# All four feature strips in one matrix call over four PSUM banks, with new orders on every engine

## What is computed

```python
x = x + tanh(g_xattn[0]) * performer(layernorm(x), ctx, ctx, random_features)   # causal, 16 heads of 8, 32 features
x = x + tanh(g_ffn[0])   * channel_mix(layernorm(x), W_r, W_k, W_v, mu_r, mu_k)   # sigmoid gate, squared relu
x = x + tanh(g_xattn[1]) * gated_cross_attention(ctx, layernorm(x), ...)   # softmax, gate by ctx @ w_la, second softmax
x = x + tanh(g_ffn[1])   * bitlinear_ffn(layernorm(x), w_gate, w_up, w_down)   # silu, rounded activations, ternary weights

# performer: the features that this change is about
q_kernel = exp(h_q + (q @ random_features - h_q))
k_kernel = exp(h_k + (k @ random_features - max(h_k)))
q_prime = (q_kernel + 1e-4) / sqrt(m); k_prime = (k_kernel + 1e-4) / sqrt(m)
```

## Time and profile before

| | |
|---|---|
| time, median of 3 runs | 516.45 us (516.07 to 518.67) |
| the profiled execution, its own time | 517.48 us |
| the profiled execution, its span | 515.7 us |
| PE busy | 457.6 us (89%) |
| DVE busy | 416.4 us (81%) |
| ACT busy | 372.6 us (72%) |
| POOL busy | 301.4 us (58%) |
| DMA | 15.15 MB, mean 29 GB/s |

### The profile page before, as it was taken

The page is one execution under the profiler, slowest core; times in us unless marked ns, Lnnn a source line. Parts: engine busy times, 40 slices in busy tenths (PEclk is TensorE's granted clock), DMA queues, the critical chain, the costliest instruction groups (busy, mean ns, idle before and its releaser), DMA issues.

```text
span 515.7 us, 19055 instructions
## 1 busy us (share of the span) xinstructions
PE 457.6 (89%) x7618; PEld 332.3 (64%) x7618; DVE 416.4 (81%) x1368; ACT 372.6 (72%) x773; POOL 301.4 (58%) x416
## 2 busy tenths in 40 slices
PE   3888889999999999999999999999999999877754
PEld 1455667676767676767677676767686767554531
DVE  2572685989889898989898989899898989888834
ACT  2455475978787878787887978797878787766633
POOL 6053356566757485857666666757484857554620
PEclk9696999999999999999999999999999999989997
DMA  5501101001010100101010101010100101000000
GB/s 201 127 3 40 37 10 35 11 4 45 11 45 11 39 18 14 41 3 52 3 50 7 49 8 46 11 45 11 43 14 21 35 2 23 1 22 3 12 11 10
DMA packets 31526, 15.15 MB, mean 29 GB/s; under 512 B 12496, under 2 KB 30800, under 8 KB 31440
## 3 DMA queue, kind: packets, MB, share of 16 engines
q1 hardware_dynamic: 30576, 13.78, 10.0%
q10 hardware_dynamic: 864, 0.16, 0.2%
HBM read 9.73 MB, written 2.10 MB: 23 GB/s over the span
## 4 chain that ended last, share of the span: by engine, by line
PE 64%; ACT 13%; DVE 8%; POOL 7%; issue 4%; DMA 2%; ACTq 1%; POOLq 0%; DVEq 0%
PE TP L1499 10%; PE MC L1532 9%; PE FP L1407 7%; PE MA L1423 6%; PE FP L1386 4%; POOL ft L402 4%; ACT ft L621 4%; ACT ft L622 3%; PE SP L1603 3%; PE SP L1490 3%; PE FP L1390 3%; PE FP L1388 3%; ACT E L658 3%; DVE WT L981 2%; DMA wla<-in_L_xattn_w_la 2%
## 5 line engine op out<-in xcount | busy, mean ns | idle before, releaser
L402 POOL TENSOR_SCALAR ft<-ft 128x512 f32<-128x512 f32 x64 | 39.5, 617 | 75.1 <-ACT ft L622 71.6
L1532 PEld LDWEIGHTS MC<-Vc,ET 128*64 128x64 f32 x2048 | 65.4, 138 | 26.3 <-issue 24.9
L1532 PE MATMUL MC<-Vc,ET 128*64 128x25 f32 x2048 | 71.6, 218 | 2.6 <-ACT ET L663 2.3
L425 POOL TENSOR_TENSOR Zn<-E,rsh 128x1024 f32<-128x1024 f32 x32 | 60.9, 1903 | 11.3 <-DVE rsh L1041 11.0
L433 POOL TENSOR_TENSOR Zn<-Zn,Gs 128x1024 f32<-128x1024 f32 x32 | 60.9, 1902 | 2.2 <-DVE Gs L1052 0.7
L669 ACT ACTIVATE ET<-TP 128x512 f32<-128x512 f32 x64 | 37.8, 595 | 25.3 <-PE TP L1499 25.3
L981 DVE TENSOR_TENSOR WT<-FP,mask 128x512 f32<-128x512 f32 x64 | 43.6, 682 | 7.7 <-PE FP L1407 7.5
L1407 PE MATMUL FP<-ft 32*64 32x64 f32 x2048 | 37.6, 221 | 12.8 <-POOL ft L402 8.7
L1407 PEld LDWEIGHTS FP<-ft 32*64 32x64 f32 x2048 | 34.1, 134 | 20.8 <-issue 18.3
L1021 DVE TENSOR_REDUCE mx<-SP 128x16 f32<-128x1024 f32 x32 | 39.0, 1220 | 6.6 <-PE SP L1490 6.5
L663 ACT ACTIVATE ET<-TP 128x512 f32<-128x512 f32 x64 | 38.0, 596 | 7.5 <-PE TP L1499 6.7
(11 more groups left out here) (202 smaller groups left out, 1187.2 us busy)
## 6 DMA issues: line engine op xcount, KB each, us to landing
Cd<-in_ctx SPq DMA_DIRECT2D x32, 128.0 KB, 2.9
kX<-kT SPq DMA_DIRECT2D x256, 8.0 KB
X<-in_x SPq DMA_DIRECT2D x16, 128.0 KB, 2.2
call<-in_ctx SPq DMA_DIRECT2D x4, 512.0 KB, 9.0
out_x<-X SPq DMA_DIRECT2D x16, 128.0 KB, 1.9
wffn<-in_L_ffn_w_gate SPq DMA_DIRECT2D x1, 256.0 KB, 4.8
wffn<-in_L_ffn_w_up SPq DMA_DIRECT2D x1, 256.0 KB, 5.3
wffn<-in_L_ffn_w_down SPq DMA_DIRECT2D x1, 256.0 KB, 6.8
```

The costliest lines, as they stand in the source:

```text
L402: pool.tensor_scalar(f, f, EPS_K, 1.0, ALU.add, ALU.mult).then_inc(s("ftp"), 1)
L425: pool.tensor_tensor(z, E1[u][:, :].rearrange("p (h m) -> p h m", m=64), rsh[u][:, :].unsqueeze(2).to_broadcast([P, H, 64]), ALU.subtract) ...
L1532: last = mm(MC[64 * j:64 * j + 64, c + 32 * q:c + 32 * q + 25], weights[:, q, 64 * j:64 * j + 64], Vc[g.p][:, 2 * u + j, q, 0:25], start=T ...
```

## The change

`features` on PE loses its argument: one call does all four strips, two into FP and two into SP, and SP's banks are the ones that the scores and the gate and up products use. ACT reads strips 2 and 3 from SP. The one wait of ACT is for all strips together, and PE's call waits for `ls` of the step's scores, that is until DVE has read the last of them. The order of the calls is new on PE, ACT, DVE and POOL, and SP spreads the keys of a group one stage earlier (b in place of c). Every call of before is still there, and its instructions have the same shapes. Several calls stand on the other side of the step's boundary now: `weights0` (first half) is called with a, `ffn0_in` and `ffn0_out` with b, `turn1` with c alone, `yD` and the row quantities of the rounding with d.

```diff
-                if c:
-                    keys_spread(c)
+                if b:
+                    keys_spread(b)
...
             def features(g, w):
 
-                at(act, s("f"), g.k * 2 + 1 + w)
-                f = FP[:, :].rearrange("p (i t n) -> p t i n", i=2, t=2)
+                if w == 0:
+                    at(act, s("f"), g.k + 1)
+                f = (FP, SP_)[w][:, :].rearrange("p (i t n) -> p t i n", i=2, t=2)
                 act.activation(ft[:, 0, 2 * w:2 * w + 2, :], f[:, 0], ACT.Exp).then_inc(s("fe"), 1)
                 act.activation(ft[:, 1, 2 * w:2 * w + 2, :], f[:, 1], ACT.Exp, bias=nkst[:, 0:1]).then_inc(s("fe"), 1)
...
-            def features(g, w):
+            def features(g):
 
                 at_ends(pe, g, s("WT"), g.k * 4)
-                if w == 0:
-                    at(pe, s("Vc"), g.k * 2)
-                    at(pe, s("csq"), g.k + 1)
-                    at(pe, s("kT"), g.k)
-                    at(pe, s("qcT"), g.k + 1)
-                elif w == 1:
-                    at_ends(pe, g, s("Vc"), g.k * 2)
-                    at_ends(pe, g, s("kT"), g.k)
-                    at(pe, s("fe"), g.k * 4 + 2)
-                strips = [(32 * i, 512 * (i % 2), i) for i in (2 * w, 2 * w + 1)]
-                for r, o, i in strips:
-                    mm(FP[:, o:o + 256], Rf[r:r + 32, i, :], qcT[r:r + 32, 0:256], start=True, stop=True)
...
+                at(pe, s("Vc"), g.k * 2)
+                at(pe, s("csq"), g.k + 1)
+                at(pe, s("kT"), g.k)
+                at(pe, s("qcT"), g.k + 1)
+                at(pe, s("ls"), g.k * 2 - 2)
+                strips = [(32 * i, (FP, SP_)[i // 2], 512 * (i % 2), i) for i in range(4)]
+                for r, bank, o, i in strips:
+                    mm(bank[:, o:o + 256], Rf[r:r + 32, i, :], qcT[r:r + 32, 0:256], start=True, stop=True)
+                for r, bank, o, i in strips:
+                    mm(bank[:, o + 256:o + 512], Rf[r:r + 32, i, :], qcT[r:r + 32, 256:512], start=True, stop=False)
+                for r, bank, o, i in strips:
+                    last = mm(bank[:, o + 256:o + 512], Nh[r:r + 32, i, :], csq[r:r + 32, :], start=False, stop=True)
                 last.then_inc(s("f"), 1)
```

More of the change, by code:

```diff
@@ L742, in step @@
                     yC(c)
+                if d:
+                    softmax2(d, 1)
+                if c:
+                    queries_in(c)
                 if e:
                     ffn_scale(e, 0)
+                if b:
+                    keys(b)
+                if c:
+                    queries(c)
+                if d:
+                    softmax2(d, 2)
+                if a:
+                    if a.k == 1:
+                        round_weights()
+                    yA(a)
+                if d:
+                    softmax2(d, 3)
+                if e:
+                    ffn_scale(e, 1)
+                    ffn_mid(e, 0)
+                if a:
+                    rows_T(a)
+                if c:
+                    gates_Tb(c)
+                if b:
+                    values1(b)
+                    yB(b)
                 if a:
@@ L1147, in step @@
             def step(a, b, c, d, e):
-                if d:
-                    least(d, 0)
-                if e:
-                    quant_max(e)
+                if b:
+                    if b.first:
+                        constants()
+                        prepare()
+                        weights_abs()
+                        weights0_turned()
+                        weights_mean()
+                    causal(b, 0)
+                    causal(b, 1)
+                if c:
+                    ffn0(c)
                 if d:
@@ L1240, in step @@
                 if b:
-                    mvB(b)
+                    gates(b)
                 if c:
-                    largest(c, 0)
+                    largest(c, 1)
+                    less(c, 1)
+                if d:
+                    attend1(d)
+                    stD(d)
+                if b:
+                    token_mix(b)
+                if d:
+                    mvD(d)
+                if c:
+                    least(c, 0)
+                    gates2(c)
+                if d:
+                    nbD(d)
+                if c:
+                    shift(c, 0)
                 if e:
@@ L1385, in features @@
-                for r, o, i in strips:
-                    mm(FP[:, o:o + 256], Rf[r:r + 32, i, :], qcT[r:r + 32, 0:256], start=True, stop=True)
-                for r, o, i in strips:
-                    mm(FP[:, o + 256:o + 512], Rf[r:r + 32, i, :], qcT[r:r + 32, 256:512], start=True, stop=False)
-                for r, o, i in strips:
-                    last = mm(FP[:, o + 256:o + 512], Nh[r:r + 32, i, :], csq[r:r + 32, :], start=False, stop=True)
+                at_ends(pe, g, s("hg"), g.k * 2 - 6)
@@ L1708, in step @@
                 if c:
[L1709 to L1715 removed]
+                    scores(c, 1)
                 if d:
                     project_T(d)
[L1718 to L1722 removed]
+                if b:
+                    if b.first:
+                        weights_turn()
+                    rows_BT(b)
                 if d:
@@ L1731, in step @@
                 if a:
-                    gates_sum(a)
+                    if a.first:
+                        constants()
+                        warm(2)
+                    features(a)
                 if c:
-                    scores(c, 1)
+                    turn1(c, 0)
+                if e:
+                    if e.k == NG - 2:
+                        warm_end(1)
+                    if e.k == NG - 1:
+                        warm_end(1)
+                    ffn_dn(e, 0)
+                if c:
+                    gates_bc(c)
+                    turn1(c, 1)
+                if b:
+                    if b.first:
+                        warm(3)
+                    ffn0_in(b)
                 if e:
@@ L1739, in step @@
                 if c:
-                    turn1(c, 0)
-                    turn1(c, 1)
-                if b:
-                    if b.first:
-                        weights_turn()
-                    rows_BT(b)
+                    turn1(c, 2)
+                    turn1(c, 3)
                 if a:
@@ L1748, in step @@
                         prepare()
-                    features(a, 1)
+                        weights_total()
+                        warm(6)
+                    weights0(a, 0)
+                if b:
+                    if b.first:
+                        warm(1)
+                    ffn0_out(b)
             run(pe, step)
```

361 lines of the change are left out of this document (137 added, 224 removed).

## The result

The changed kernel takes 554.61 us (median of 4 runs, 550.58 to 558.06), the kernel before beside it 516.26. The ratio is 1.073, 95% interval 1.065 to 1.082: slower by 7%, where the prediction said 503 us and faster. Its profiled execution took 553.16 us with a span of 551.4.

A forecast was written before the change was run, and what follows sets the result against it. Step bound by PE now, by the bank readers' chain over ACT and POOL after the change. Span 515.7 + 4.0 - 12.7 - 4.9 = 502.1, time 503 us; range for 8 in 10: 494 to 515.

The forecast's parts named there:

- All four strips: Features call on PE: four strips overlap fully, 1.55 us for the one call, 1.5 us saved per step.
- the rival in which they don't overlap: Features on PE: strips do not overlap four wide, call 3.0 us, time 521.5 us, slower; 8 in 100.
- The full step is 26.5: Each of twelve full steps takes 26.5 us, 1.05 less than now; 12.7 us saved in all.
- the walk: One new step followed along the new order from the first L1407 (t = 0) to the next, at 26.5 us.
- The rival of the closed places: DVE or ACT operation 0.5 us late in the full step: step 27.2 to 27.4, time 511 to 514; 17 in 100.
- forecast 14.4 to 14.7: Full step, PE's stretch from L1407 to the end of the fourth turn2: 14.4 to 14.7 us.
- the 24.9 forecast: PE's own work in a full step falls from 26.4 to 24.9 us.
- 0.3 to 0.6: Full step: PE waits 0.3 to 0.6 us for POOL ahead of L1407.
- Forecast +4.0: Filling: net 4.0 us lost, as later rounding delays clipping; -2 if clipping is hidden, 6 if rows_BT slips more.
- the 3.32 of the earlier trace: Filling: clipping on DVE taken as 3.32 us, running 39.1 to 42.4 instead of 35.14 to 38.5.
- Forecast -4.9: Draining: 4.9 us saved, give or take 3, called the least checked part.
- the forecast was 42.5: Draining, from the last group's first L1407 to its last subtraction: 42.5 us, against 48.4 before.

The follow-up runs named there:

- one_input_both: Changed kernel, no added waits; Gs a reciprocal straight from PSUM, rsh the largest of emn alone (gate factor and pos left out): 517.4 us, ratio 1.000.
- own_operands: Changed kernel's whole computation, no added waits, neither Gs nor rsh a product of two SBUF operands, weights rounded early: 516.9 us, ratio 0.999.
- gs_wait: Changed kernel with one added wait: POOL's subtraction of d's second half waits for DVE's second Gs; 530.1 us, ratio 1.026.

## Why the prediction was wrong

**The features.** All four strips took 1.5 us in one call, as forecast, and the rival in which they don't overlap fell. Its price was off as well: two pairs right behind each other take 2.0 us and not 3.0, so that of the 1.5 us saved about 1.0 comes from standing together and 0.5 from four strips side by side.

**The full step.** "The full step is 26.5" was the step that failed, and in it an assumption that the walk makes without writing it down: that DVE's small operations cost in their new places what they cost in the old ones. The second `rsh` and the second `Gs` have no term in it. The new order puts the second `rsh` and the second `Gs` beside POOL's subtractions of 1.9 us, and each is held to the subtraction's end: 1.3 to 1.7 us instead of 0.2 to 0.3. The profiles' spans miss the forecast by 551.4 - 502.1 = 49.3 us; the steps have 354.1 - 318.0 = 36.1 of it. Against one_input_both, 32.2 are the held products: twelve times 28.88 - 26.83 = 24.6, and six times 30.15 - 28.88 = 7.6 for the clock that falls in PE's wait behind them. The other 3.9 us are 26.83 against 26.5, of which one step with 27.66 is 1.0. So the walk over PE, ACT and POOL was right to 0.2 us in an ordinary step. What it did not ask is which work of POOL runs beside two of DVE's smallest instructions.

The trace of before had shown it. `Gs` read 252 ns in the median and 1061 at the longest, for the same 16 elements, and the prediction counted neither value nor asked what the long ones stood beside. The rival of the closed places had DVE late by 0.5 us, a step of 27.2 to 27.4 and at worst the time of the kernel before; the two products are late by about 1.1 and 1.5 us in the chain.

**The bound of the full step.** Without the held products the chain of an ordinary step in one_input_both is PE's up to the fourth `turn2`, 14.9 us (forecast 14.4 to 14.7), and ACT's and POOL's from there, 11.8, in which PE has work but is not what the end waits for. So the readers of the banks bound the second part, and the step is 26.70 where PE's own work is 25.2 (302.55 in twelve steps) and not the 24.9 forecast. It is close: PE stands idle only 0.14 us ahead of L1395, where the forecast had 0.3 to 0.6. The Trainium skill ("TensorEngine Tiling (Array Packing)", Performance Considerations) warns that emptying PSUM may be the bottleneck after a fourfold tiling; one_input_both agrees for this second part.

**The filling.** Forecast +4.0, measured +5.6, by two errors of opposite sign. The clipping took 1.47 us and not the 3.32 of the earlier trace rows; the 3.32 had POOL's memset beside it (33.97 to 37.52 in the kernel before), so a row was carried to a place where its neighbour is another. Below, the memset of the kernel before and the clipping of the changed one, whose memset is over at 37.1:

```profile
33.97 3.55 POOL L331 MEMSET kX<- 128x2048 f32 x2
```

```profile
37.88 1.47 DVE L869 TENSOR_SCALAR wtb<-wt 128x512 bf16<-128x512 f32 x3 [5.29 <-ACT wt L544]
```

L1395 of the second group came at 53.1 and not 55.2. But the step behind it took 25.8 and not 22.8, since the features now wait for both scores to be read, in a chain of scores, largest, subtraction, twice over (64.5 to 72.0 in one_input_both), and the features then run at half the clock (2.9 us); the next step took 25.4 and not 24.7. That the rounding's place matters was right, and POOL's memset in the chain was missed.

**The draining.** Forecast -4.9, measured +6.7. Of the 11.6 us between the two the held products have 3.3 (93.0 against 89.7 in one_input_both). The other 8.3 us are the walk's. From the last group's first `weights0` to its last subtraction the forecast was 42.5; one_input_both has 47.2 and the kernel before 48.4. Behind it the forecast was 38.9, measured 42.5 (before 37.9). In this stretch PE waits for DVE's order of scores, statistics and `ffn_out`, and its clock is at half in parts of it. Moving `ffn_out` did not shorten the profiled stretch, and the fillers are worth 1.8 us by the medians, hardly clear of the noise. How the 8.3 divide between order and clock stays open.

## What to carry to other kernels

When an order moves instructions of DVE beside other work of POOL, look at the operands before the durations: in these traces a DVE product with two operands in SBUF that started beside a POOL instruction reading SBUF ended with that instruction, however small it was itself. Take the minimum, median and maximum of each small group in the trace, and find what the longest one stands beside; that spread is the price of a wrong neighbour. It is removed by leaving one operand in PSUM, by laying both in one tile for a reduction, or by a wait on POOL, where POOL has the room.

## What the runs showed of the hardware

A held product ends 0.02 or 0.03 us behind POOL's instruction, in all 56 cases of the changed kernel's trace (POOL's instructions of 0.62, 0.73 and 1.90 us). A reciprocal straight from PSUM kept its 0.25 us inside the same subtraction (one_input_both), a product with one operand in PSUM its 0.17 (own_operands), and a reduction from SBUF its 1.20 beside POOL's additions. One operand is no safe conduct, though: the bf16 clipping, with a single SBUF operand, took 3.32 us beside a POOL memset that only writes and 1.47 or 1.06 us without one; that was seen in traces and not tried by itself. And a wait of PE of 0.9 to 1.4 us in every step cost another 1.27 us in half of the steps, through the clock, which fell in no full step once the wait was gone (gs_wait).
